# Two-layer sandwich block: the loop over pairs of batches begins at the first slot of an instruction block

## What is computed

```python
q, k, v = x @ Wq, x @ Wk, x @ Wv
latent_kv = (k + v) @ W_down_kv
k_rec, v_rec = latent_kv @ W_up_k, latent_kv @ W_up_v
...
scores = jnp.einsum('bhqd,bhkd->bhqk', qh, kh) * scale
...
scores = scores * decay[None, None, :, :]
...
attn = jax.nn.softmax(scores, axis=-1)
out = jnp.einsum('bhqk,bhkd->bhqd', attn, vh)
...
x = x + _layernorm(_L0_attn_ref(_layernorm(x, axis=-1), Wq, Wk, Wv, Wo, W_down_kv, W_up_k, W_up_v), axis=-1)
x = x + _layernorm(_L0_ffn_ref(_layernorm(x, axis=-1), weight), axis=-1)
```

## Time and profile before

| what | value |
|---|---|
| median of 3 runs | 1533.29 us (1532.9 to 1538.11) |
| the profiled execution | 1533.83 us |
| its span, first to last instruction | 1532.0 us |
| TensorE matmul busy | 1334.8 us, 87% |
| VectorE busy | 1195.0 us, 78% |
| ScalarE busy | 1139.8 us, 74% |
| GpSimd busy | 828.9 us, 54% |
| mean granted clock of TensorE | 0.954 of full speed |

### The profile page before, as it was taken

The page is one execution under the profiler, slowest core; times in us unless marked ns, Lnnn a source line. Parts: engine busy times, 40 slices in busy tenths (PEclk is TensorE's granted clock), DMA queues, the critical chain, the costliest instruction groups (busy, mean ns, idle before and its releaser), DMA issues.

```text
span 1532.0 us, 37259 instructions
## 1 busy us (share of the span) xinstructions
PE 1334.8 (87%) x12850; PEld 589.4 (38%) x12850; DVE 1195.0 (78%) x2743; ACT 1139.8 (74%) x1225; POOL 828.9 (54%) x1244
## 2 busy tenths in 40 slices
PE   5889999898898989989898998989989898999963
PEld 3334344343343434434343433334434343444332
DVE  7568888788887878878787887878878787887645
ACT  1878888677787868878787786868877787788841
POOL 4234556456555556646456555546646456556446
PEclk9899999999999999999999999999999999999976
DMA  5545555555555564545565455554555565465420
GB/s 182 162 142 178 161 170 178 163 174 155 161 167 157 167 195 122 174 151 177 162 191 155 144 177 150 175 184 141 158 154 171 162 195 153 143 191 167 140 73 28
DMA packets 174666, 243.24 MB, mean 159 GB/s; under 512 B 28336, under 2 KB 145200, under 8 KB 174512
## 3 DMA queue, kind: packets, MB, share of 16 engines
q1 hardware_dynamic: 140176, 206.78, 43.6%
q10 hardware_dynamic: 34336, 34.08, 7.6%
HBM read 154.80 MB, written 69.21 MB: 146 GB/s over the span
## 4 chain that ended last, share of the span: by engine, by line
PE 42%; issue 14%; DVE 11%; ACT 10%; DMA 10%; SPq 7%; POOL 5%; ACTq 1%; DVEq 0%; POOLq 0%
PE heads_ps L763 15%; PE scores_ps L750 9%; PE misc_ps L679 8%; ACT probs L968 7%; SPq L510 6%; DMA den_scratch<-den_inv 5%; DMA den_spread<-den_scratch 4%; POOL heads_c L1110 4%; DVE diagonal L1342 4%; PE misc_ps L721 3%; DVE x_hl L1293 2%; ACT probs L975 1%; DVE weighted L1250 1%; PE misc_ps L693 1%; PE misc_ps L651 1%
## 5 line engine op out<-in xcount | busy, mean ns | idle before, releaser
L968 ACT ACTIVATE probs<-scores_ps 128x1024 f32<-128x1024 f32 x768 | 756.9, 1029 | 287.0 <-PE scores_ps L750 286.9
L763 PE MATMUL heads_ps<-probs,v_sb 128*32 128x512 f32 x4096 | 537.9, 615 | 4.1 <-DVE heads L1239 3.3
L750 PE MATMUL scores_ps<-q_rep,k_rep 64*128 64x128 f16 (+2 forms) x5120 | 333.6, 254 | 64.1 <-DVE diagonal L1342 26.4
L1342 DVE TENSOR_TENSOR diagonal<-scores_ps,comp 128x1024 f32<-128x1024 f32 x256 | 311.8, 1218 | 90.9 <-PE scores_ps L750 88.8
L750 PEld LDWEIGHTS scores_ps<-q_rep,k_rep 64*128 64x128 f16 x5120 | 164.9, 95 | 400.2 <-DVE diagonal L1342 143.9
L1063 POOL TENSOR_TENSOR ln_neg_mean<-zero,ln_moments 128x4 f32<-128x4 f32 (+1 forms) x131 | 26.3, 201 | 434.9 <-DVE ln_moments L1191 434.7
L975 ACT ACTIVATE probs<-diagonal 128x2048 f32<-128x2048 f32 x128 | 245.8, 1920 | 0.0
L1250 DVE SCALAR_TENSOR_TENSOR weighted<-misc_ps,edges 128x384 f32<-128x384 f32 x256 | 128.5, 543 | 38.8 <-PE misc_ps L651 21.3
L1110 POOL TENSOR_TENSOR heads_c<-heads_c,den_spread 128x1024 f32<-128x1024 f32 (+1 forms) x33 | 76.5, 2319 | 145.4 <-DMA den_spread<-den_scratch 145.4
L763 PEld LDWEIGHTS heads_ps<-probs,v_sb 128*32 128x32 f32 x4096 | 91.9, 109 | 158.0 <-issue 156.1
L679 PE MATMUL misc_ps<-wo,heads_c 128*128 128x256 f32 x504 | 125.9, 393 | 21.3 <-POOL heads_c L1110 21.2
(11 more groups left out here) (150 smaller groups left out, 1611.7 us busy)
## 6 DMA issues: line engine op xcount, KB each, us to landing
q_rep<-q_scratch SPq DMA_DIRECT2D x128, 384.0 KB, 4.2
k_rep<-k_scratch SPq DMA_DIRECT2D x256, 192.0 KB, 3.6
q_scratch<-q_hl SPq DMA_DIRECT2D x64, 384.0 KB, 2.6
k_scratch<-k_hl SPq DMA_DIRECT2D x64, 384.0 KB, 3.1
x_in<-in_L_attn_x_dram ACTq DMA_DIRECT2D x32, 512.0 KB, 5.5
heads_c<-heads SPq DMA_DIRECT2D x256, 64.0 KB, 2.9
x_res<-in_L_attn_x_dram ACTq DMA_DIRECT2D x32, 512.0 KB, 6.2
den_spread<-den_scratch SPq DMA_DIRECT2D x256, 64.0 KB, 2.3
```

The costliest lines, as they stand in the source:

```text
L750: ins = mm(scores_ps[:, place + par, at:at + n * P], k_rep[rows, pair, kv_, k_cols], q_rep[rows, pair, qv_, q_cols], start=True, stop=True)
L763: ins = mm(heads_ps[W32 * g:W32 * (g + 1), :], v_sb[:, b.slot, kt, at:at + W32], probs[:, quad % 2, g, kt, :], start=(kt == 0), stop=(kt = ...
L968: nc.scalar.activation(flat[:, :, at:at + S], scores_ps[:, place:place + 2, :], ACT.Exp, scale=EXP_SCALE).then_inc(off_probs, 1)
L1342: v.tensor_tensor(diagonal[:, quad % 2, 2 * two:2 * two + 2, :], scores_ps[:, place:place + 2, :], comp[:].rearrange("p t n -> p (t n)").u ...
```

## The change

The loop of every engine is opened with a wanted place for its head. The call pads the engine's code so that the loop's first instruction is loaded at slot 0 of a block of 256 instruction slots, and the padding is jumped over when the loop is entered. The body stays the same.

```diff
             for i in range(4):
                 one(i)
-            with eng.Fori(0, (B - 6) // 2) as loop:
+            with nc.Fori(0, (B - 6) // 2, engines=[eng.engine], head_slot={eng.engine: 0}) as loop:
                 if enter_loop is not None:
                     enter_loop(loop, Batch(loop, 4, 2))
                 iteration(loop, 4, everything)
```

## The result

The changed kernel takes 1453.24 us in the median of 4 runs (1449.96 to 1454.08), the kernel before 1533.84 us beside it: a ratio of 0.9465, 95% interval 0.9442 to 0.9489. That is 80.6 us less, where 64.8 were forecast.

The account below looks back on a forecast made before the run. TensorE was taken to bound the kernel, stalled by instruction loading at back-edges. Saving 5.4 us at each of 12 (91.71 to 86.3 per pair), 64.8 us, with entry and other engines 0: 1533.8 - 64.8 = 1469 us, range 1459 to 1501.

Parts of the forecast that it names:

- TensorE sets the pace and loses two gaps per back-edge to instruction loading: TensorE's loop: busy 82.17 of 91.71 us per pair, idle 1.69 and 3.05 us around each back-edge, waiting for instruction blocks.
- Head 35 slots ahead of a block's end, eight blocks spanned, nine loaded: TensorE's loop body: 1730 instructions span eight blocks of 256, and with one fetched ahead nine are reloaded every pair.
- Seven blocks and the one ahead are kept: TensorE's aligned loop: if eight blocks are kept, the branch finds its block and both gaps go; 64.8 us saved, chance 0.67.
- Gaps 52.9 us, slow clock about 12: TensorE's back-edges: gaps of 32.9 and 20.0 us in total, plus about 1 us of slow clock per pair.
- Waits for others that recur each batch, as heads_c, are inside these periods and stay: TensorE's loop: recurring waits, such as 19.2 us for heads_c, lie within the 43.16 us batch periods and remain.
- The bound of 42.76 us: Shortest den_inv period without a back-edge; taken for every batch, it put the saving at 74 us.
- Entry costs 0 to 4 us, other engines nothing: Loop entry: jumping the padding taken as 0, with 4 us in the range; other engines' aligned branches change by 0 us.
- Signs of being right: At all 12 back-edges TensorE's branch under 0.2 us, almost no loop packets, den_inv periods near 43.2 us, clock at upper level.
- the first: TensorE's back-edge: the branch still misses, only the second gap goes; 1489 to 1501 us, taken as 1495, chance 0.22.
- The second: TensorE's loop head: the mark does not move it as the hardware counts blocks; 1533 us, chance 0.07.
- third: Other engines' back-edges: their branches begin to miss, 0 to 46 us slower, taken as 1557 us, chance 0.04.
- The fourth: Loop without gaps: another wait takes over as ScalarE, GpSimd and DMAs cannot catch up; within 1481 us, inside the 0.67.

Follow-up runs that it names:

- Slot 221: Changed kernel with TensorE's loop head at block slot 221, its inferred earlier place, other engines at 0: 1531.8 us, ratio 0.9998 to the kernel before.
- slot 160: Changed kernel with TensorE's loop head at block slot 160, other engines at 0: 1490.19 us, ratio 0.9735 to the kernel before.
- Slot 62: Changed kernel with TensorE's loop head at block slot 62, other engines at 0: 1455.09 us, ratio 0.9512 to the kernel before.
- slot 80: Changed kernel with TensorE's loop head at block slot 80, other engines at 0: 1512.51 us, ratio 0.9877 to the kernel before.
- slot 63: Changed kernel with TensorE's loop head at block slot 63, other engines at 0: 1455.5 us, ratio 0.9508 to the kernel before.

## Why the prediction was wrong where it was, and right where it was

- *TensorE sets the pace and loses two gaps per back-edge to instruction loading*: right. Slot 221 brings both back, slot 160 the first alone.
- *Head 35 slots ahead of a block's end, eight blocks spanned, nine loaded*: right, by slot 221.
- *Seven blocks and the one ahead are kept*: right. Slot 62 keeps all, slot 80, one block more, loads nine at every back-edge. So TensorE keeps eight blocks and not nine; only slot 63, where ten of 12 back-edges hit, is left without an account. The Trainium skill ("Advanced Engine Details and Errata", ISA Cache) has 128KB for TensorE in lines of 16KB, which is eight, and the traces agree. Its "Only 2 cache lines!" does not hold for this engine: with two, the branch would miss at slot 0 too.
- *Gaps 52.9 us, slow clock about 12*: right in size. Slot 160 leaves 12.2 for the clock. The stretch of the earlier trace rows is one of three short ones, though: at the nine other back-edges the clock stood at 0.50 for 6.8 us, not 3.4. Less of the slow clock reaches the end than the 27 us by which TensorE's busy time fell (986.09 - 959.05).
- *"Waits for others that recur each batch, as heads_c, are inside these periods and stay"*: this is the step that failed. They went, 19.2 to 1.5 us. I took the periods without a back-edge, 43.16 us, for a TensorE that is not disturbed. They were disturbed: in 20 of 24 batches a packet of TensorE's own instruction loading ran beside den_spread and made heads_c, and the output projection that waits for it, about 1 us late. Loading fewer packets was seen as removing stalls at the branch alone. The bound of 42.76 us came from batches ahead of the loop, which are written out and load packets as well, so it was no bound; the undisturbed period is 42.5. The sum by its parts is 52.9 + 12 + 17 = 82 us, against 81.6 measured in the 12 pairs; as 12 and 17 are remainders of the same two differences, what supports them from outside is the late den_spread, 13 to 16 us.
- *Entry costs 0 to 4 us, other engines nothing*: right. The jump took TensorE 0.32 us, and the other engines' branches stay at 45 to 56 ns.
- *Signs of being right*: TensorE's branch is 0.215 us or a little more at the back-edges, just over the 0.2 named, and the periods are 42.5 us, not 43.2.
- Rivals: the first was the state of slot 160, 1490 us beside a before of 1533.5, inside its 1489 to 1501, though it carries the 17 us and next to no slow clock. The second and third did not come about. The fourth holds in part: the waits for diagonal rose from 14.2 to 29.5 us, while those for heads_c, which the forecast held fixed, gave way by 17.7.

## What to carry to other kernels

When one engine alone has a branch of microseconds at a loop's end, count its instructions to the block and count its packets per round: one block too many reloaded the whole body here, and another place of the head that saves the block, slot 62, was as good as slot 0. Price a stall by a state that lacks its cause everywhere, not by the quiet stretches of the same trace, since these may pay for the cause too. What a late chain of small DMAs costs is read by making it late on purpose, a little more each time: here the first 0.27 us cost nothing, the next step did.

## What the runs showed of the hardware that was not expected

- A 16 KB instruction packet beside eight small DMAs delays their end by about 1 us (6.57 against 5.54 us to heads_c), as long as most packets run. The delay lies in one of the sync engine's eight issues, which takes 0.95 to 2.04 us instead of 0.42. Which resource they share was not tried.
- TensorE's code written out without a loop is a little slower than a loop that finds its blocks, 1461.7 against 1453.2 us, or 3 to 8 us in the loop's time.
- One gap of 1.7 us at the back-edge left the granted clock at its upper level in 11 of 12 cases; a gap of 2.6 us took it to 0.50 in 7 of 12, and the two gaps of 1.7 and 2.7 us, with about 1 us of work between them, in all 12.
